# Two layers of attention and feed-forward on one core: the second layer's entrance put in another order

## The reference

```python
x = L0_attn_x
xn = _layernorm(x, axis=-1)
x = x + _L0_attn_ref(xn, ...) + _L0_ffn_ref(xn, ...)
xn = _layernorm(x, axis=-1)
x = x + _L1_attn_ref(xn, ...) + _L1_ffn_ref(xn, ...)
return x
```

```python
h = x
for blk in range(3):
    i0, i1 = (2 * blk, 2 * blk + 1)
    y = _qlora_linear(h, qweights[i0], scales[i0], biases[i0], lora_a[i0], lora_b[i0])
    y = _layernorm(y, ln_gamma[blk], ln_beta[blk])
    y = jax.nn.gelu(y, approximate=False)
    y = _qlora_linear(y, qweights[i1], scales[i1], biases[i1], lora_a[i1], lora_b[i1])
    h = y + h
return h
```

## Time and profile before

| | us |
|---|---|
| time, median of 3 runs | 1180.4 |
| lowest and highest of them | 1179.7, 1180.87 |
| the profiled execution's own time | 1181.08 |
| its span | 1179.3 |
| PE busy | 1155.9 |
| DVE busy | 990.5 |
| ACT busy | 811.3 |
| POOL busy | 408.3 |

### The profile page before, as it was taken

How to read it: one execution, slowest core, us unless ns; L and a number is a source line. 1 busy time by engine, 2 the same in 40 slices (tenths; PEclk the granted TensorE clock), 3 DMA queues, 4 the chain that set the end, 5 groups by cost and what they waited for, 6 DMA issues and landing times.

```text
span 1179.3 us, 23925 instructions
## 1 busy us (share of the span) xinstructions
PE 1155.9 (98%) x8908; PEld 893.6 (76%) x8908; DVE 990.5 (84%) x1918; ACT 811.3 (69%) x2182; POOL 408.3 (35%) x364
## 2 busy tenths in 40 slices
PE   8999999999999999999999999999999999999998
PEld 6777777777776777787768777877787767777776
DVE  5988598878887888788878887888798878998887
ACT  6885577557755775677567756775677668777775
POOL 1317430650064006400640054005400658635831
PEclk9999999999999999999999999999999999999989
DMA  8004300320032003200420032003200420000000
GB/s 264 2 30 142 95 1 21 129 71 2 23 128 69 1 22 129 69 2 19 134 67 2 20 121 79 1 23 122 76 2 29 128 64 1 2 19 19 1 10 29
DMA packets 44293, 63.93 MB, mean 54 GB/s; under 512 B 8144, under 2 KB 18384, under 8 KB 43920
## 3 DMA queue, kind: packets, MB, share of 16 engines
q1 hardware_dynamic: 44176, 62.39, 16.5%
HBM read 59.48 MB, written 2.88 MB: 53 GB/s over the span
## 4 chain that ended last, share of the span: by engine, by line
PE 84%; DVE 7%; ACT 3%; issue 2%; DMA 1%; POOL 1%; SPq 1%; DVEq 0%; ACTq 0%; POOLq 0%
PE psum L1562 14%; PE psum L1581 13%; PE psum L1503 11%; PE psum L64 9%; PE psum L66 9%; PE psum L65 9%; PE psum L1618 5%; PE psum L1516 2%; PE psum L1528 2%; PE psum L1819 2%; PE psum L1585 1%; PE psum L1883 1%; DVE probs L1240 1%; ACT probs L809 1%; PE psum L1455 1%
## 5 line engine op out<-in xcount | busy, mean ns | idle before, releaser
L767 ACT ACTIVATE probs<-psum,mneg 128x256 f32<-128x256 f32 (+3 forms) x400 | 187.3, 486 | 110.6 <-DVE mneg L1173 110.3
L1562 PE MATMUL psum<-ident,probs 128*128 128x128 f32 x1600 | 211.4, 277 | 4.1 <-ACT probs L809 4.0
L1173 DVE TENSOR_REDUCE mneg<-psum 128x2 f32<-128x1024 f32 (+3 forms) x256 | 194.0, 819 | 13.9 <-PE psum L1516 11.4
L1562 PEld LDWEIGHTS psum<-ident,probs 128*128 128x128 f32 x1600 | 179.5, 142 | 31.6 <-ACT probs L767 8.4
L1164 DVE COPY pt<-psum 128x512 f32<-128x512 f32 x256 | 164.9, 683 | 38.0 <-PE psum L1562 36.1
L574 POOL TENSOR_TENSOR qk_lo<-sg,qk_hi 128x512 fp32r<-128x512 f32 x64 | 92.0, 1443 | 159.7 <-ACT qk_hi L838 159.7
L1581 PE MATMUL psum<-pt,v_all 128*64 128x384 f32 (+5 forms) x1088 | 142.6, 412 | 0.0
L538 POOL TENSOR_TENSOR rstd<-var,mhalf 128x4 f32<-128x4 f32 x7 | 7.1, 1011 | 379.8 <-DVE var L1059 379.8
L1581 PEld LDWEIGHTS psum<-pt,v_all 128*64 128x64 f32 (+1 forms) x1088 | 69.7, 135 | 62.7 <-issue 50.2
L64 PE MATMUL psum<-xt_hi,gu_hi 128*128 128x512 f32 x272 | 110.5, 406 | 0.0
L66 PE MATMUL psum<-xt_hi,gu_lo 128*128 128x512 f32 x272 | 108.1, 397 | 0.0
(11 more groups left out here) (288 smaller groups left out, 2771.2 us busy)
## 6 DMA issues: line engine op xcount, KB each, us to landing
crow<-weights SPq DMA_DIRECT2D x256, 128.0 KB, 2.9
rrow<-sums SPq DMA_DIRECT2D x128, 128.0 KB, 3.0
gu_raw<-in_gu SPq DMA_DIRECT2D x1, 2176.0 KB, 11.4
x_all<-in_x SPq DMA_DIRECT2D x8, 256.0 KB, 6.5
out_rows<-x_all SPq DMA_DIRECT2D x7, 256.0 KB, 2.3
down_raw<-in_down SPq DMA_DIRECT2D x1, 1088.0 KB, 13.5
wqkv_raw<-in_wqkv SPq DMA_DIRECT2D x1, 896.0 KB, 6.7
wqkv_raw<-in_wqkv SPq DMA_DIRECT2D x1, 512.0 KB, 4.9
```

The lines of the kernel that those rows point to most:

```text
L767: last = act.activation(probs[:, h * HALF + PROB[t]:h * HALF + PROB[t] + w], bank[score_bank(rnd, c) + h][:, o:o + w], ACT.Exp, bias=mneg[ ...
L1173: last = dve.tensor_reduce(mneg_h[:, :, t], psum[:, b:b + 2, o:o + P * (t + 1)], AX, ALU.max, negate=True)
L1562: last = nc.tensor.transpose(dst[:, i * P:(i + 1) * P], probs[:, v:v + P], ident[:, :])
```

## The change

No computation is added or left out; instructions are put in another order, use other banks and wait for other counters.

- The last linear output (`last_out(g, half)`) comes in two halves of two tiles, laid between other work; that of the group's fourth batch uses bank 7 (`ffn_bank`) and moves into the first odd pair, and so does its `take_ffn`.
- The first even pair's turned groups go to banks 4, 5, 0, 1, 7 (before 2, 3, 0, 1, 7), the first odd pair's chunk 0 to banks 2 and 3 (before 4 and 5). Its products now stand ahead of the even pair's turned groups, chunk 2 of the even pair is reduced and exponentiated after the odd pair's chunk 0, and its turned group 4 moves behind `products_beside` of the odd pair.
- `square_qk(3)` moves ahead of `take_ffn(0)`, `inv_norms(1, 1)` ahead of `inv_sqrt(2, 2)`.
- `turn_acc(B - 1)` and `add_rows(B - 1)` move into the feed-forward part of group 0.
- Between the groups, `turn_rows(q + 1, 0)` moves ahead of the last two turned groups, `weigh_batch` ahead of `turn_rows(q + 1, 1)` and `lin_in(q + 1, 0, 0)`, and ACT copies first and loads its table later; in group 1 `take_qkv1(1)` goes ahead of `gelu(0, 2)`.

```diff
-            return bank[([2, 3, 4, 7, 7] if k % (2 * G) else [2, 3, 0, 1, 7])[s]]
+            return bank[([2, 3, 4, 7, 7] if k % (2 * G) else [4, 5, 0, 1, 7])[s]]
...
+        def ffn_bank(g):
+
+            return bank[7] if g == G - 1 else bank[g]
...
-            return 4 if k % (2 * G) == 1 and c == 0 else SCORE_BANK[c]
+            return 2 if k % (2 * G) == 1 and c == 0 else SCORE_BANK[c]
...
+                inv_norms(1, 1)
                 inv_sqrt(2, 2)
                 inv_sqrt(2, 3)
-                inv_norms(1, 1)
                 norm_qk(1)
...
+                if q:
+                    take_qkv1(1)
                 gelu(0, 2)
-                take_qkv1(1)
+                if q == 0:
+                    take_qkv1(1)
...
+                if q + 1 < GROUPS:
+                    take_ht(q + 1, 0)
                 take_tile1_1(2 * (n0 + G) - 1)
+                take_sums1(n0 + G - 1)
                 if q + 1 < GROUPS:
                     load_table(ACT.Gelu)
-                    take_ht(q + 1, 0)
-                take_sums1(n0 + G - 1)
-                if q + 1 < GROUPS:
                     take_ht(q + 1, 1)
...
                 row_maxima1(2 * n0, 0)
+                square_qk(3)
                 take_ffn(0)
                 take_ffn(1)
-                square_qk(3)
                 row_maxima1(2 * n0, 1)
                 take_ffn(2)
-                take_ffn(3)
...
+                def last_out(g, half):
+
+                    pe.wait_ge(gt_ready, (q * BLOCKS + BLOCKS - 1) * G + g + 1)
+                    if half == 0:
+                        mm(ffn_bank(g), bias_on[0:96, :], bias_bf[0:96, NLIN - 1, :].unsqueeze(1).to_broadcast([96, TILES, D]), start=True, stop=False, **K)
+                    for t in range(half * TILES // 2, (half + 1) * TILES // 2):
                         c = slice(t * P, (t + 1) * P)
-                        mm(bank[g][:, c], ht[g][:, c], ident[:, :], is_transpose=True, start=False, stop=False, **K)
-                        last = mm(bank[g][:, c], gt[g][:, c], lin[:, NLIN - 1, :], start=False, stop=True, **K)
-                    last.then_inc(ffn_done, 1)
+                        mm(ffn_bank(g)[:, c], ht[g][:, c], ident[:, :], is_transpose=True, start=False, stop=False, **K)
+                        last = mm(ffn_bank(g)[:, c], gt[g][:, c], lin[:, NLIN - 1, :], start=False, stop=True, **K)
+                    if half:
+                        last.then_inc(ffn_done, 1)
...
+                if q == 0:
+                    turn_acc(B - 1)
                 lin_in(q, 2, 0)
                 lin_out(1, 1)
                 turn_norm(1, 2)
+                if q == 0:
+                    pe.wait_ge(x1_ready, B)
                 turn_k(0)
...
-                lin_out(2, 0)
-                lin_out(2, 1)
+                last_out(0, 0)
+                last_out(0, 1)
                 turn_norm(2, 2)
+                last_out(1, 0)
                 turn_norm(2, 3)
+                last_out(1, 1)
+                last_out(2, 0)
...
-                lin_out(2, 2)
+                last_out(2, 1)
+                pe.wait_ge(gt_ready, (q * BLOCKS + BLOCKS) * G)
                 turn_q(1)
-                lin_out(2, 3)
                 turn_k(1)
...
-                    for g in range(2, G):
-                        pe.wait_ge(ffn_ready, n0 + g + 1)
+                    pe.wait_ge(ffn_ready, n0 + 3)
+                    tile_products1(k + 1, 0, 3)
+                    masks1(k + 1, 0).then_inc(scored1[0], 1)
+                    pe.wait_ge(qk_lo_ready, (ROUNDS0 + n0 + 1) * 2 + 2)
                     turn1(k, 1)
                     turn1(k, 0)
-                    pe.wait_ge(qk_lo_ready, (ROUNDS0 + n0 + 1) * 2 + 2)
-                    tile_products1(k + 1, 0, 3)
-                    masks1(k + 1, 0).then_inc(scored1[0], 1)
                     pe.wait_ge(exp1_done[1][1], k + 1)
+                    pe.wait_ge(exp1_done[1][0], k + 1)
                     turn1(k, 3)
-                    pe.wait_ge(exp1_done[1][0], k + 1)
                     turn1(k, 2)
-                    for h in range(2):
-                        pe.wait_ge(exp1_done[2][h], k + 1)
-                    turn1(k, 4)
...
-                            pe.wait_ge(exp1_done[0][h], k + 1)
+                            pe.wait_ge(exp1_done[2][h], k)
+                        turn1(k - 1, 4)
+                        pe.wait_ge(pt1_ready[0], k)
+                        pe.wait_ge(pt1_ready[1], k)
...
-                    elif q == 0:
+                    else:
                         pe.wait_ge(pt1_ready[4], k)
-                        turn_acc(B - 1)
+                        last_out(G - 1, 0)
+                        last_out(G - 1, 1)
...
+                    if g == G - 1 and q + 1 < GROUPS:
+                        turn_rows(q + 1, 0)
...
-                if q + 1 < GROUPS:
-                    turn_rows(q + 1, 0)
                 pe.wait_ge(pt1_ready[4], 2 * (n0 + G))
                 turn_sums1(n0 + G - 1)
                 if q + 1 < GROUPS:
+                    weigh_batch(G - 1)
                     turn_rows(q + 1, 1)
                     lin_in(q + 1, 0, 0)
-                    weigh_batch(G - 1)
```

More of the change, by code:

```diff
@@ L1015, in _ @@
                             round_k(ROUNDS0 + n0 + g + 1)
[L1016 to L1019 removed]
+                    if g:
+                        exps1(ka, 1, 1)
+                        exps1(ka, 1, 0)
+                        exps1(ka, 2, 0)
+                        exps1(ka, 2, 1)
                     exps1(kb, 0, 1)
                     exps1(kb, 0, 0)
+                    if g == 0:
+                        exps1(ka, 2, 0)
+                        exps1(ka, 2, 1)
                     if g:
@@ L1355, in _ @@
                 stats1(q, 1, 3)
+                if q == 0:
+                    add_rows(B - 1)
                 add_hidden(1, 1)
@@ L1407, in _ @@
                         add_attention(g - 1)
-                    elif q == 0:
-                        add_rows(B - 1)
+                    else:
+                        take_ffn(G - 1)
                     take_turned1(kb, [1])
@@ L1435, in _ @@
                     norm_rows1(n0 + G, G - 2)
-                    stats1(q + 1, 0, 0)
                 dve.wait_ge(y_done, ROUNDS0 + n0 + G)
@@ L1440, in _ @@
                 if q + 1 < GROUPS:
+                    stats1(q + 1, 0, 0)
                     stats1(q + 1, 0, 1)
@@ L2040, in odd_pair @@
                 def odd_pair(k, g):
-                    pe.wait_ge(pt1_ready[0], k)
-                    pe.wait_ge(pt1_ready[1], k)
+                    if g:
+                        pe.wait_ge(pt1_ready[0], k)
+                        pe.wait_ge(pt1_ready[1], k)
+                    else:
+                        for h in range(2):
+                            pe.wait_ge(exp1_done[0][h], k + 1)
                     masks1(k, 1, True)
```

43 lines of the change are left out of this document (20 added, 23 removed).

## The result

| | runs | median, us | ratio to before, 95% interval |
|---|---|---|---|
| before | 16 | 1180.12 (1178.27 to 1182.37) | |
| after | 16 | 1183.05 (1180.70 to 1185.14) | 1.0021 (1.0014 to 1.0028) |

The prediction was 1178.8, with a range up to 1182.2. The kernel became 2.9 us slower instead of 1.6 us faster. The profiled execution of after took 1184.29 us (span 1182.4).

A forecast was written before the change was run, and what follows sets the result against it. PE's order was taken to bound the kernel. Gains of 0.35 and 0.55 us at the entrances and 1.0 between the groups, 1.9 in all, less 0.3 for one clock fall, gave 1178.8 us, range 1175.9 to 1182.2.

The forecast's parts named there:

- the clock: At the second layer's entrances: PE's clock falls once in either kernel, costing 2.1 us before and 2.4 after.
- two falls: Rival: waits close together make the clock fall at both entrances, 2.4 us each, giving 1181.2; chance 0.18.
- the slower one: Rival: at the entrances the clock stays down half as long again, 3.9 us a fall, two falls giving 1184.2; chance 0.10.
- no fall: Rival: the longest single wait shrinks from 1.23 to 0.8 us, the clock holds at the entrances, giving 1176.4; chance 0.26.
- The sum at a full clock: Whole change at an unchanged clock: 0.35 us from group 1's entrance, 0.55 from group 0's, 1.0 between the groups, 1.9 gained.
- Up to the masks: Entrance, up to the masks of chunk 1: they start at 1111.6 (bounds 1111.2 and 1112.2) instead of 1110.28.
- POOL's later `nmr` stretches the entrance: Entrance: named sign of being wrong; nmr of the third and fourth batch was expected some 0.6 us later.
- the clash: Entrance, DVE's square_qk(3) against POOL: if it goes on, masks near 1111.8, without it near 1111.3, 0.5 us an entrance.
- Masks to `products_beside`: Entrance, masks of chunk 1 to the odd pair's products_beside: 8.4 us instead of 11.08, so 1.3 earlier than before.
- To the next even pair: Entrance, from products_beside to the next even pair: 7.5 us at a full clock, against 6.55 before in group 1.
- `turn_acc`: Group 0, moved into the feed-forward part: mostly hidden there, costing 0.1 us, or 0.4 more if that cover is missing.
- Between the groups: Between the groups: waits worth at most 1.55 us go, new ones of 0.3 and about 0.3 come; gain 1.0 (bounds 0.3, 1.55).

The follow-up runs named there:

- e_linin: After with unread products filling the first odd pair's three waits, inv_norms(1, 1) back behind inv_sqrt(2, 3), lin_in(1, 0, 0) ahead of weigh_batch(3), stats1 ahead of y1t: 0.9974 of before, 1176.91 us.
- e_between: The kernel before with only the edits between the groups: ratio to before 0.9999.
- e_acc: The kernel before with only turn_acc and add_rows of batch 7 moved into the feed-forward part, turn_k(0) behind them: ratio to before 1.0003.
- e_entrance: The kernel after with the edits between the groups undone, so the entrance part alone: ratio to before 1.0028.
- e_inv_back: The kernel after with one line put back, POOL's inv_norms(1, 1) behind inv_sqrt(2, 3) again: ratio to before 1.0010.

## Why the prediction was wrong

**The step that failed is the clock.** The prediction charged one fall to either kernel, 2.1 us before and 2.4 after, because the one profiled execution of before showed one. By the mean clock the old order has it in 45 of 108 runs (0.996 or less), the new one in 16 of 16. The mean clock says 1180 x (0.9970 - 0.9949) = 2.5 us more lost than before, where 0.3 was written. Not all lost clock costs time: 3.4 us lost cost 2.2 in the old order and 3.1 in the new. An estimate by these prices, 3.1 in every run against 2.2 in 45 of 108, is 2.2 us. That the new order has less idle time to absorb a fall was seen rightly, but charged at 2.4 us. The rival "two falls", held to be half as likely, came nearer (1181.2), as did the slower one (1184.2), though neither has the mechanism right: after's profile shows one fall at an entrance, not two, and the clock stayed down no longer than before (6.8 us in both); it was dearer than supposed, and above all it came in every run. That the longest wait shrank from 1.23 to 0.86 us, which "no fall" leaned on, did not help: three waits within 3.5 us were worse. Filling them gave back 3.2 us.

**The sum at a full clock.** Predicted 1.9 us of gain, found 0.06: 0.03 in group 0 for 0.55, a loss of 0.37 in group 1 for a gain of 0.35, 0.40 between the groups for 1.0.

- *Up to the masks:* 5.47 us were written (1111.6 - 1106.13), 5.72 measured. By PE's work alone it should be 5.04, and with POOL's line put back it is 5.02. The step named the right cause, POOL's 2.27 us, and "POOL's later `nmr` stretches the entrance" among its signs of being wrong, but charged 0.4 for it, and it costs 0.7, since `nmr` also ran into `square_qk(3)`. The Trainium skill (SBUF — State Buffer, section Who interferes with whom) has a VectorE instruction with two SBUF inputs and a GpSimd one that reads SBUF shut each other out for a whole instruction; by that rule `nmr` waits for the multiplication, and 0.83 us, ending with it, agrees. The prediction's number for the clash, masks at 1111.8, came (1106.13 + 5.72 = 1111.85), but it looked for it at the wrong end: the multiplication itself shows 0.95 us, not 1.79, and the one held up is POOL.
- *Masks to `products_beside`:* 8.51 for 8.4. The waits were 0.86 and 0.67 for 0.8 and 0.8. Right (DVE's terms as written add to 3.9, not 3.8, which makes it 8.5).
- *To the next even pair:* 7.79 for 7.5, with the wait ahead of turned group 4 at 0.63 for 0.6. What it is measured against was 0.13 too high (6.42, not 6.55): group 1 was worked out from group 0 less the 0.29 in the bracket of the wait for `add_rows`, and that wait costs 0.42.
- *`turn_acc`:* hidden, 19.41 us instead of 19.40 (980.92 to 1000.33 in after). Right, though it was hidden in its old place too.
- *Between the groups:* the wait ahead of `turn_norm(0, 0)` was put at 0.3 and is 0.78; `e_linin` shows that it is this chain.

With all of that the result closes within its interval (1181.8 to 1183.4): 1180.12 - 0.06 + 2.5 = 1182.6, or 1182.3 by the prices, measured 1183.05. The last half microsecond is not accounted for.

**What would have shown it beforehand.** More runs of the kernel before with their mean clocks. Three profiles with the same old entrance in group 1, those of before, `e_between` and `e_acc`, show one fall and two times none. The prediction took one profile for the habit of the kernel. The Trainium skill (TensorE: Matmul & The Clock Gate, Part 1) sets the clock by how busy PE has been recently. The windows agree as far as each fall comes behind waits (1.85 us busy of 4.00), but the same 1.84 of 4.00 in group 1 brought none. The prediction read that page as speaking against the change and gave the case 18 in 100; the direction was right, but after's profile has one fall at its entrances, not two.

## What to carry to other kernels

Where PE is the bound, judge a reordering also by how closely PE's waits lie together, not only by its longest wait: here three waits of 0.86, 0.67 and 0.63 us within 3.5 us cost more clock than two of 1.23 and 1.22 farther apart. Read the mean clock of many runs before pricing a fall, since a single profile shows one draw; and if waits cannot be taken away, a few unread products into a free bank are a cheap test and here also a cure. When an order is changed on one engine, look for waits inside merged rows (four transposes in 1.38 us instead of 0.60), and for the small instruction on POOL that now runs beside a two-input one on DVE.

## What was not expected of the hardware

- The clock fell to 1.2 GHz although PE had been busy for 1.85 of the 4.0 us ahead (after, group 0), and did not fall behind exactly the same pattern in group 1. It stayed down for about 6.8 us in which PE was busy throughout.
- A 128 x 4 instruction on POOL took 0.83 us instead of 0.20 beside a 128 x 768 multiplication on DVE that has both inputs in SBUF, while the same multiplication beside POOL's powers of 128 x 12 took its own 0.95 us.
- Every fall seen lost either 1.7 or 3.4 us of full clock, 22 falls in 14 profiles, and nothing between.
- In the first layer every profile shows a fall that begins between 115 and 118 us, behind a stretch with little work (in before PE was busy for 2.67 of the 4.00 us from 112 on), and it loses 1.7 or 3.4 us with the same code. What decides between the two, and why the fall in the second layer chose group 0 in after, `e_entrance` and `e_inv_back` alike, stays open.
